# Gate and up products of the last feed-forward: full fp32 products, or three products of split parts

## The chip, the cores and the metric

The kernel runs as one program on one core of a Trainium2 chip. The metric is the device time of one execution in microseconds (us), lower being better. The engines are TensorE (PE: matmuls and transposes through the array, with its weight loads listed apart as PEld), VectorE (DVE), ScalarE (ACT), GpSimd (POOL) and SyncE (SP, which here issues the DMAs).

## What is computed

Four layers, each a cross attention and a feed-forward with a residual and a layer norm, over x of 4 x 256 tokens with 256 features. The change is in the last feed-forward, which multiplies operands that were rounded to 8-bit floats in blocks of 32, each with a scale of its own:

```python
def _mx_dequant(t):            # blocks of 32 along the last dimension
    max_abs = jnp.max(jnp.abs(blocks), axis=-1)
    scales = jnp.maximum(max_abs / 448.0, 1e-30)
    q = (blocks / scales[..., None]).astype(jnp.float8_e4m3fn).astype(jnp.float32)
    return (q * scales[..., None]).reshape(rows, feat)

def _mx_linear(x2d, w):
    return _mx_dequant(x2d) @ _mx_dequant(w).T

gate = _mx_linear(x2d, gate_w)          # 1024 tokens x 256 -> 1024
up = _mx_linear(x2d, up_w)              # 1024 tokens x 256 -> 1024
h = jax.nn.silu(gate) * up
out = _mx_linear(h, down_w)             # 1024 -> 256
```

Before it stands the last cross attention, a linear attention with a sigmoid gate and an output projection; its tokens are worked on in four batches of 256.

## The kernel before

Each engine has one program, written out by hand, and runs it in its written order; semaphores join them. What matters here is the end of each program.

**The last attention** is a loop over four batches b = 0 to 3. In one pass PE makes the denominators and the attention of b, projects query and gate of b + 1 (`query_and_gate`), spreads the inverse denominators over the heads (`spread`, line 1486), transposes a third of the last feed-forward's weights (`pe_turn(pe, "l3", ...)`, b = 1 gate, b = 2 up, b = 3 down; line 475), and projects the output. ACT makes the exponential and the sigmoid of b (lines 1956 and 1963) and then copies the transposed weights out of PSUM (`copy_out`, line 489); PE may run two groups of transposes ahead of these copies. DVE makes the inverse denominators (lines 2718 to 2720), the shares and the product (2729, 2733), the next query's features (2708) and adds the projected output into `x_t` (2742). GpSimd has rounded the weights earlier.

**Before the feed-forward** PE transposes the first 512 tokens back to token rows (line 1537), ACT copies them (1977), DVE rounds them (`tokens_quantised(0)`, through `mx_quant`, lines 2199 to 2216, with `ln_xc_of` 2059 between its steps), PE transposes them again (`quantised_turned`, line 1544) and ACT copies them into `xq_t` (`quantised_copied`, line 1983).

**The feed-forward** goes over eight tiles t of 128 tokens. `gate_up(t)` makes gate into PSUM banks 0 and 1 and up into banks 2 and 3: four outputs of 512 columns, each a sum over KC = 2 products of a 128 x 128 token tile and 128 x 512 weights, thus 8 products a tile. There is one set of these four banks, so `gate_up(t)` waits for the product of tile t - 1 (`m_mul`). ACT applies silu to the gate (`gate_act`, line 1998), DVE multiplies (`product`, line 2766) and rounds the hidden tile (`mx_quant`), GpSimd puts the scale back on (line 933), PE transposes it (`hidden_turned`, line 1573), ACT copies it (line 2005), PE makes `down(t)` of 8 products with 256 columns each, and DVE adds the residual (`result`, line 2790). PE's order in pass t is hidden_turned(t), down(t - 1), gate_up(t + 2); DVE's is product(t + 2) with its rounding, then result(t). The last tile is handled in two halves (lines 2780, 1596, 2017). The tokens of the second half are rounded on DVE after product(1) (`tokens_quantised(1)`) with their last steps on GpSimd (937, 938, 933), and are transposed in PE's pass t = 2, in two pieces around hidden_turned(2) and down(1). All matmuls pass through the helper `mm`, line 959.

Of the kernel before, what the change touches and what calls it, by code (L numbers as in the profile page):

```python
# [13 lines left out]
ALU = mybir.AluOpType  # L14
# [10 lines left out]
P = 128  # L25
D = 256
# [37 lines left out]
def build(nc, a, out, stop=None):  # L64
# [5 lines left out]
    with ExitStack() as ctx:  # L70
# [3 lines left out]
        def sem(name):  # L74
            return ctx.enter_context(nc.semaphore(name))
# [134 lines left out]
        def part_weights(b):  # L210
# [81 lines left out]
        lx_share = c([KC, SEQ])  # L292
        lx_o = c([2, KC, SEQ])
        c = Cut(c3.at / 256)
        wt_l3 = [c([KC, H3]), c([KC, H3]), c([8, D])]
        assert c.at / 256 <= late_at
        c = Cut(0)
        mxq = c([8 * D])
        mx_s = c([2, 96])
        xn_tok = c([TT, D])  # L300
        xq_t = c([KC, TOK])
        h_tok = c([2, H3])
        h_act = c([H3])
        hq_t = c([2, 8, P])
        x_tok = c([TT, D])
        res = c([2, D])


        dve_step, act_step, pool_step = sem("dve_step"), sem("act_step"), sem("pool_step")
# [39 lines left out]
            "lx_made", "lx_copied", "lx_min_r", "lx_exp_r", "lx_keys", "lx_sum", "lx_bd"))  # L349
        lx_qg, lx_qmin_r, lx_act, lx_qf, lx_dens, lx_inverse, lx_att, lx_or, lx_x = (sem(n) for n in (  # L350
            "lx_qg", "lx_qmin_r", "lx_act", "lx_qf", "lx_dens", "lx_inverse", "lx_att", "lx_or", "lx_x"))
        xt_turned, xt_copied, xq_ready, xq_turned, xq_copied = (sem(n) for n in (
            "xt_turned", "xt_copied", "xq_ready", "xq_turned", "xq_copied"))
        res_copied = sem("res_copied")
        m_gu, m_act, m_mul, m_ht, m_htc, m_o, m_res = (sem(n) for n in (
            "m_gu", "m_act", "m_mul", "m_ht", "m_htc", "m_o", "m_res"))
        stored = [sem("stored_even"), sem("stored_odd")]
# [40 lines left out]
        def mark(name, f):  # L398
            first = len(groups)
            f()  # L400
            marks[name] = (first, len(groups))
# [22 lines left out]
        def three(ws, wts, h, wait, fixed):  # L424
            turn_in(h, ws[0], wts[0], wait, fixed)
            turn_in(h, ws[1], wts[1], wait, fixed)
            turn_out(h, ws[2], wts[2], wait, fixed)
# [12 lines left out]
            turn_in(D, lx_nat[1], lx_t[1], (load["l3x"], 16 * 5), 0)  # L440
            turn_in(D, lx_nat[2], lx_t[2], (load["l3x"], 16 * 5), 0)
        mark("lx", lx)
        mark("l3", lambda: three(w_l3, wt_l3, H3, (mx_fixed, 12), 0))

        by_dve = [g % 2 == 1 and not marks["l1"][0] <= g < marks["small"][1] and g < marks["l3"][0] for g in range(len(groups))]

# [510 lines left out]
        def _(pe):  # L957
# [590 lines left out]
            def gate_up(t):  # L1548


                if t:
                    pe.wait_ge(m_mul, t)
                else:
                    pe.wait_ge(xt_copied, 2)
                    pe.wait_ge(res_copied, 2)
                pe.wait_ge(xq_copied, 2 * (t // 4) + 2)
                for n in range(4):

                    j, c2_ = divmod(n, 2) if t < TT - 1 else (n % 2, n // 2)
                    for k in range(KC):  # L1560
                        last = mm(ps[:, 2 * j + c2_, :], xq_t[:, k, t * P:(t + 1) * P],
                                  wt_l3[j][:, k, c2_ * 512:(c2_ + 1) * 512], k == 0, k == KC - 1)
                    if n % 2 or t == TT - 1:
                        last.then_inc(m_gu, 1)

            def hidden_turned(t):

# [9 lines left out]
            def down(t):  # L1577
                pe.wait_ge(m_htc, t + 1)

                if t == 0:  # L1580
                    pe.wait_ge(res_copied, 4)
                elif t < TT - 2:
                    pe.wait_ge(m_res, t)
                for k in range(8):
                    last = mm(ps[:, down_bank(t), 0:D], hq_t[:, t % 2, k, :], wt_l3[2][:, k, :], k == 0, k == 7)
                last.then_inc(m_o, 1)
# [37 lines left out]
            gate_up(1)  # L1624
            for t in range(TT - 1):
                if t == 2:
                    pe.wait_ge(res_copied, 4)
                    quantised_turned(1, 0, 7)
                hidden_turned(t)

                if t:
                    down(t - 1)
                else:
                    pe.wait_ge(xt_copied, 4)
                    tokens_turned_back(x_t, 1, (6, 7))
                if t == 2:
                    pe.wait_ge(xq_copied, 3)
                    quantised_turned(1, 1, 7)
                if t + 2 < TT:
                    gate_up(t + 2)  # L1640
# [8 lines left out]
        def _(act):  # L1649
# [300 lines left out]

            copy_out(act, "lx", False)
            ln_sq_of("l3x", 1)
            act.wait_ge(load["l3x"], 16 * 5)
            for b in range(BATCH):
                act.wait_ge(lx_qmin_r, b + 1)
                act.activation(lx_qmin[:, b % 2], lx_qmin[:, b % 2], ACT.Exp).then_inc(lx_act, 1)
                if b == 0:
                    ln_sd_of("l3x", 1)
                act.wait_ge(lx_qg, 2 * b + 2)
                if b >= 2:  # L1960
                    act.wait_ge(lx_or, b - 1)
                for o in range(KC):
                    last = act.activation(lx_gate[:, b % 2, o, :], ps[:, 1, o * SEQ:(o + 1) * SEQ], ACT.Sigmoid,
                                          bias=bg[:, o:o + 1])
                last.then_inc(lx_act, 1)
                if b == 3:
                    ln_sd_of("l3", 0)
                if b:
                    copy_out(act, "l3", False, (b - 1, BATCH - 1))
                if b == 2:  # L1970
                    ln_sq_of("l3", 0)
# [8 lines left out]
            def quantised_copied(n, bank):  # L1980
                h, k = divmod(n, 2)
                act.wait_ge(xq_turned, n + 1)
                act.activation(xq_t[:, k, tok(h)], ps[:, bank, :], ACT.Copy).then_inc(xq_copied, 1)

            for k in range(KC):
                tokens_copied(k, xn_tok, k, xt_copied)
            for k in range(KC):
                tokens_copied(2 + k, x_tok, 2 + k, res_copied)
            ln_sq_of("l3", 1)
            ln_sd_of("l3", 1)  # L1990
            for k in range(KC):
# [27 lines left out]

            gate_act(0)  # L2020
            for k in range(KC):
                tokens_copied(4 + k, xn_tok, 6 + k, xt_copied)
            for t in range(1, TT - 1):
                gate_act(t)
                if t == 3:
                    quantised_copied(2, 7)
                hidden_copied(t - 1)
                if t == 1:
                    for k in range(KC):
                        tokens_copied(6 + k, x_tok, 6 + k, res_copied)  # L2030
                if t == 3:
                    quantised_copied(3, 7)
            last_gate(0)
# [7 lines left out]
        def _(dve):  # L2041
# [661 lines left out]
            def query_features(b):  # L2703
                dve.wait_ge(lx_act, 2 * b + 1)
                if b >= 2:
# [2 lines left out]
                STT(lx_q[:, b % 2], ps[:, 0, :].rearrange("p (k t) -> p k t", k=KC), 0.0, lx_qmin[:, b % 2], ALU.max,  # L2708
                    ALU.add).then_inc(lx_qf, 1)

            query_negative(0)
            query_features(0)
            ln_diag_of("l3x", 1)
            for b in range(BATCH):
# [28 lines left out]
                if b % 2:  # L2743
                    dve.wait_ge(lx_x, b + 1)
                    dve.sem_inc(x_ready, 1)


            def tokens_quantised(h, **parts):
# [2 lines left out]
                return mx_quant(v, mxq[:, 4 * D * h:4 * D * h + 4 * D], mx_s[:, 0, 64:96], mx_s[:, 1, 64:96], 32, step,  # L2751
                                **parts)

            dve.wait_ge(xt_copied, 2)
            tokens_quantised(0, between=lambda: ln_xc_of("l3", 1)).then_inc(xq_ready, 1)
            ln_diag_of("l3", 1)
            ln_xn_of("l3", 1)

            def product(t):
# [31 lines left out]

            product(0)
            product(1)
            dve.wait_ge(xt_copied, 4)
            dve.wait_ge(xq_ready, 1)
            tokens_quantised(1, rounded=False).then_inc(xq_ready, 1)
            for t in range(TT - 2):
                if t < TT - 3:
                    product(t + 2)
                else:  # L2800
                    last_product(0)
                    last_product(1)
                result(t)
            result(TT - 2)
            result(TT - 1)

# [27 lines left out]
```

## Time and profile before

| | us |
|---|---|
| median of 3 runs | 1015.25 (1014.58 to 1015.99) |
| the profiled execution, whole | 1018.44 |
| its span in the trace | 1016.7 |
| PE busy, share of the span | 864.5 (85%) |
| DVE busy | 716.9 (71%) |
| ACT busy | 453.4 (45%) |
| GpSimd busy | 164.7 (16%) |

All times of single instructions are from this one profiled execution, in microseconds from the start of its span. A busy share is a mean over stages with different limits; the stage of the change is the last 130 us, and is read there by itself. PE's clock is granted at one of two levels, 2.4 GHz (shown as 1.00) and 1.2 GHz (0.50); its mean over this execution is 0.837.

### The profile page before, as it was taken

The page shows a single profiled execution, that of the slowest core. Times are in us where ns is not written, and L with a number is a line of the kernel's source. Part 1 is how long each engine was busy: PE and PEld are TensorE (multiplying, and loading weights), DVE is VectorE, ACT ScalarE, POOL GpSimd, SP SyncE. Part 2 cuts the span into 40 slices and gives each one's busy share as a digit, 9 for nine tenths or more (in the row PEclk, how much of TensorE's full clock was granted, in tenths as well). Part 3 has the DMA queues.
Part 4 walks back from the last instruction along what each step waited for, and adds up shares of the span by engine and source line. Part 5 has one row for each costly group of instructions (what it writes and reads, how often), then busy time and mean ns, then how long its engine had stood idle before and what let it go on. Part 6 is the DMA issues. An engine that isn't in the chain of part 4 may idle for free.

```text
span 1016.7 us, 11697 instructions
## 1 busy us (share of the span) xinstructions
PE 864.5 (85%) x4246; PEld 515.2 (51%) x4246; DVE 716.9 (71%) x962; ACT 453.4 (45%) x695; POOL 164.7 (16%) x251
## 2 busy tenths in 40 slices
PE   5989894489889999999899777777778989889898
PEld 3434662244645555554455434444445657754566
DVE  1776558964457887777668898889985545358777
ACT  2214446642324332222123499888995434532111
POOL 1000000000005424333400062111110000001412
PEclk9899885579979999999899955555558999979999
DMA  8602002100132222141021899987771100000000
GB/s 264 201 2 46 1 0 46 24 2 7 15 50 38 34 33 36 43 65 16 0 47 20 168 170 162 167 154 128 141 140 32 32 0 1 1 1 1 10 11 21
DMA packets 211612, 59.14 MB, mean 58 GB/s; under 512 B 192398, under 2 KB 209892, under 8 KB 211556
## 3 DMA queue, kind: packets, MB, share of 16 engines
q1 hardware_dynamic: 211444, 58.23, 29.8%
q8 instruction: 34, 0.56, 0.2%
q10 hardware_dynamic: 112, 0.17, 0.1%
q14 instruction: 22, 0.18, 0.1%
HBM read 20.62 MB, written 1.05 MB: 21 GB/s over the span
## 4 chain that ended last, share of the span: by engine, by line
PE 55%; DVE 25%; ACT 9%; issue 8%; DMA 1%; POOL 1%; ACTq 1%; DVEq 0%; POOLq 0%
PE ps L959 50%; DVE arena L2640 2%; ACT xc L1924 2%; PE ps L1402 2%; DVE arena L2274 1%; PE ps L475 1%; ACT sq L1924 1%; DVE arena L2204 1%; PE ps L1090 1%; DVE xc L2446 1%; ACT arena_split L1839 1%; DVE sq L2553 1%; DVE sq L2550 1%; DVE xn_t L2075 1%; DVE arena L2188 1%
## 5 line engine op out<-in xcount | busy, mean ns | idle before, releaser
L959 PE MATMUL ps<-arena 128*128 128x16 f16 (+8 forms) x1776 | 265.5, 320 | 50.6 <-ACT xc L1924 22.1
L959 PE MATMUL ps<-arena_split 128*128 128x512 f32 (+6 forms) x736 | 200.4, 436 | 18.6 <-DVE arena_split L2452 5.7
L959 PEld LDWEIGHTS ps<-arena 128*128 128x128 f16 (+4 forms) x1776 | 131.9, 129 | 157.7 <-issue 101.8
L959 PEld LDWEIGHTS ps<-arena_split 128*128 128x128 f32 (+6 forms) x736 | 134.8, 196 | 91.0 <-issue 40.8
L2640 DVE TENSOR_REDUCE arena<-ps 128x1 f32<-128x1024 f32 x128 | 152.3, 1220 | 18.6 <-PE ps L959 17.5
L1924 ACT ACTIVATE xc<-ps,arena 128x1024 int16<-128x1024 f32 x86 | 103.2, 1207 | 13.0 <-POOL arena L916 12.5
L959 PE MATMUL ps<-sq,arena 128*64 128x256 f32 (+3 forms) x256 | 80.9, 515 | 8.0 <-DVE sq L2553 8.0
L865 POOL TENSOR_SCALAR arena<-arena 128x512 f32<-128x512 f32 x12 | 23.1, 1922 | 249.5 <-DVE arena L2468 249.5
L916 POOL TENSOR_SCALAR arena<-arena 128x1 f32<-128x1 f32 x128 | 33.9, 264 | 182.1 <-DVE arena L2640 181.8
L1691 ACT ACTIVATE act_buf<-ps 128x512 f32<-128x512 f32 (+2 forms) x34 | 20.3, 597 | 90.9 <-PE ps L959 90.8
L959 PE MATMUL ps<-mean_w,sq 128*128 128x1 f32 x240 | 35.2, 277 | 21.3 <-ACT sq L1656 21.3
L1924 ACT ACTIVATE sq<-ps,arena 128x1024 int16<-128x1024 f32 x42 | 50.5, 1207 | 5.7 <-POOL arena L916 5.5
L959 PEld LDWEIGHTS ps<-sq,arena 128*64 128x64 f32 (+3 forms) x256 | 30.1, 166 | 43.2 <-issue 31.2
L959 PEld LDWEIGHTS ps<-mean_w,sq 128*128 128x128 f32 x240 | 35.0, 229 | 29.5 <-ACT sq L1656 27.6
L933 POOL TENSOR_TENSOR arena<-arena 128x1024 f32<-128x1024 f32 (+1 forms) x9 | 17.5, 1949 | 186.3 <-DVE arena L2212 186.1
L959 PE MATMUL ps<-x_t,mean_w 128*128 128x512 f32 x64 | 37.9, 723 | 7.8 <-DVE x_t L2296 4.3
L959 PE MATMUL ps<-xn_t,arena 128*128 128x256 f32 (+2 forms) x112 | 39.9, 505 | 0.0
L2384 DVE TENSOR_TENSOR hid_buf<-ps,act_buf 128x512 f32<-128x512 f32 (+2 forms) x18 | 12.4, 690 | 33.8 <-ACT act_buf L1691 33.5
L1830 ACT ACTIVATE act_buf<-ps 128x512 f32<-128x512 f32 x16 | 9.6, 599 | 56.4 <-PE ps L959 56.4
L1839 ACT ACTIVATE arena_split<-xc 128x1024 fp32r<-128x1024 f32 x16 | 16.9, 1059 | 39.3 <-DVE xc L2446 39.3
L475 PE MATMUL ps<-ident,arena 128*128 128x128 f32 (+4 forms) x122 | 22.8, 344 | 13.6 <-DMA arena<-in_x 6.5
L2452 DVE TENSOR_TENSOR arena_split<-xc,arena_split 128x1024 fp32r<-128x1024 f32 x16 | 21.1, 1317 | 18.7 <-ACT arena_split L1839 18.7
(298 smaller groups left out, 1344.5 us busy)
## 6 DMA issues: line engine op xcount, KB each, us to landing
arena<-in_L_ffn_w SPq DMA_DIRECT2D x4, 640.0 KB, 6.0
arena_split<-arena_split SPq DMA_DIRECT2D x59, 32.0 KB
arena<-in_x SPq DMA_DIRECT2D x1, 1024.0 KB, 5.6
arena<-in_ctx SPq DMA_DIRECT2D x1, 1024.0 KB, 8.0
arena<-in_L_xattn_Wkv SPq DMA_DIRECT2D x2, 512.0 KB, 4.0
arena<-in_L_ffn_gate_w SPq DMA_DIRECT2D x1, 1024.0 KB, 10.3
arena<-in_L_ffn_up_w SPq DMA_DIRECT2D x1, 1024.0 KB, 12.8
arena<-in_L_ffn_down_w SPq DMA_DIRECT2D x1, 1024.0 KB, 12.5
```

The source lines that it names most:

```text
L475: last = pe.transpose(ps[0:m, 6 + g % 2, col:col + w], src, ident[0:src.shape[0], 0:src.shape[0]])
L865: step(pool.tensor_scalar(qf, qf, 2.0 ** -6, 1.5 * 2.0 ** 20, ALU.max, ALU.mult))
L916: pool.tensor_scalar(A["bias"][:, b:b + 1], A["nm"][:, b:b + 1], A["sq"][:, t, i:i + 1], math.log(255.0), ALU.mult, ALU.add).then_inc(att_ ...
L933: return pool.tensor_tensor(v, v, scale.unsqueeze(2).to_broadcast([P, n, MX_BLOCK]), ALU.mult)
L959: return pe.matmul(o, l, r, start=start, stop=stop)
L1402: last = pe.transpose(ps[:, 7, :].bitcast(BF16)[:, k * P:(k + 1) * P], y[:, k * P:(k + 1) * P], ident_b[:, :])
L1691: act.activation(act_buf[0:r, u % 2, :], ps[0:r, 2 * (u % 2), :], func, scale=1.0 if scale is None else scale[0:r, :]).then_inc(act_ready, 1)
L1839: act.activation(moe["xe_parts"][:, n % 2, 0], moe["xe"], ACT.Copy).then_inc(moe_xh, 1)
L1924: act.activation(probs(u).rearrange("p (a b) -> p a b", a=2), ps[:, score_banks(u), :], ACT.Exp, bias=att_small["bias"][:, u % 3:u % 3 + 1 ...
L2384: return TTN(hid, up, s, ALU.mult)
L2452: TTN(parts[:, n % 2, 1], moe["xe"], parts[:, n % 2, 0], ALU.subtract).then_inc(moe_xl, 1)
L2640: dve.tensor_reduce(A["nm"][:, b:b + 1], ps[:, score_banks(u), :], AX.XY, ALU.max, negate=True).then_inc(att_max, 1)
```

## The change

Gate and up become three products of parts. Each weight matrix and the rounded tokens are split into a high part, which is the value as ScalarE writes it into the type float32r (`fp32r` in the trace), and a low part, which is the value less the high part, by VectorE, again in float32r. Then x w is made as x_high w_high + x_high w_low + x_low w_high, 24 products a tile in place of 8. The products of `down` stay as they were.

The transposed gate and up weights are first copied to `w3_turned`. In the attention's loop `weight_high(b - 2)` (two ScalarE instructions of 128 x 1024) and `weight_low(b - 2)` (two VectorE instructions of 128 x 1024) stand in passes b = 2 (gate) and b = 3 (up). The tokens' low parts are four VectorE instructions of 128 x 512, `quantised_low`, of which two stand ahead of the first tile, one after result(0), and one after product(3), ahead of result(1). The copies `quantised_copied` write the high parts in place of the plain values. In the first tile of each half (t = 0 and 4) the products with the low part of the tokens come last of all, so that tile's first `m_gu` comes after 20 of its 24 products.

```diff
-        wt_l3 = [c([KC, H3]), c([KC, H3]), c([8, D])]
+        wt_l3 = [c([KC, H3], F32R), c([KC, H3], F32R), c([8, D])]
...
-        xq_t = c([KC, TOK])
+        xq_high = c([KC, TOK], F32R)
...
+        xq_rest = c([KC, TOK], F32R)
+        assert c.at <= c3.at
+        w3_turned = Cut(late_at)([2, KC, H3])
+        w3_rest = Cut(late_at)([2, KC, H3], F32R)
...
@@ gate_up(t), tensor @@
-                    pe.wait_ge(xt_copied, 2)
-                    pe.wait_ge(res_copied, 2)
-                pe.wait_ge(xq_copied, 2 * (t // 4) + 2)
-                for n in range(4):
-
+                    pe.wait_ge(tok_copied, 4)
+                pe.wait_ge(l3_high, WEIGHTS3 + 2 * (t // 4) + 2)
+                pe.wait_ge(l3_low, WEIGHTS3)
+                late = t % 4 == 0
+                if not late:
+                    pe.wait_ge(l3_low, WEIGHTS3 + 2 * (t // 4) + 2)
+                x, y = xq_high[:, :, t * P:(t + 1) * P], xq_rest[:, :, t * P:(t + 1) * P]
+
+                def columns(n):
                     j, c2_ = divmod(n, 2) if t < TT - 1 else (n % 2, n // 2)
+                    return ps[:, 2 * j + c2_, :], j, slice(c2_ * 512, (c2_ + 1) * 512)
+
+                def leading(n):
+                    o, j, at = columns(n)
                     for k in range(KC):
-                        last = mm(ps[:, 2 * j + c2_, :], xq_t[:, k, t * P:(t + 1) * P],
-                                  wt_l3[j][:, k, c2_ * 512:(c2_ + 1) * 512], k == 0, k == KC - 1)
+                        mm(o, x[:, k, :], wt_l3[j][:, k, at], k == 0, False)
+                        mm(o, x[:, k, :], w3_rest[:, j, k, at], False, False)
+
+                def remaining(n):
+                    o, j, at = columns(n)
+                    for k in range(KC):
+                        last = mm(o, y[:, k, :], wt_l3[j][:, k, at], False, k == KC - 1)
                     if n % 2 or t == TT - 1:
                         last.then_inc(m_gu, 1)
+
+                for n in range(4):
+                    leading(n)
+                    if not late:
+                        remaining(n)
+                if late:
+                    pe.wait_ge(l3_low, WEIGHTS3 + 2 * (t // 4) + 2)
+                    for n in range(4):
+                        remaining(n)
...
@@ the attention's loop, scalar @@
+            def weight_high(j):
+
+                act.wait_ge(*copied(marks["l3"][0] + 4 * j + 3))
+                for k in range(KC):
+                    act.activation(wt_l3[j][:, k, :], w3_turned[:, j, k, :], ACT.Copy).then_inc(l3_high, 1)
+
...
                 if b == 3:
                     ln_sd_of("l3", 0)
+                if b >= 2:
+                    weight_high(b - 2)
                 if b:
                     copy_out(act, "l3", False, (b - 1, BATCH - 1))
...
@@ the attention's loop, vector @@
+            def weight_low(j):
+
+                for k in range(KC):
+                    dve.wait_ge(l3_high, KC * j + k + 1)
+                    TTN(w3_rest[:, j, k, :], w3_turned[:, j, k, :], wt_l3[j][:, k, :], ALU.subtract).then_inc(l3_low, 1)
+
...
                 if b % 2:
                     dve.wait_ge(lx_x, b + 1)
                     dve.sem_inc(x_ready, 1)
+                if b >= 2:
+                    weight_low(b - 2)
...
+            def quantised_low(n, bank):
+                h, k = divmod(n, 2)
+                dve.wait_ge(l3_high, WEIGHTS3 + n + 1)
+                TTN(xq_rest[:, k, tok(h)], ps[:, bank, :], xq_high[:, k, tok(h)], ALU.subtract).then_inc(l3_low, 1)
+
...
             ln_diag_of("l3", 1)
+            for k in range(KC):
+                quantised_low(k, 4 + k)
             ln_xn_of("l3", 1)
...
+                if t == 1:
+                    quantised_low(3, 7)
                 result(t)
+                if t == 0:
+                    quantised_low(2, 7)
```

The rest of the diff renames semaphores (`xt_copied` and `res_copied` become one counter, `tok_copied`; `xq_copied` becomes `l3_high`) with the counts that belong to them, and lets PE's second piece of `quantised_turned` in pass t = 2 wait for quantised_low(2), which reads the same PSUM bank.

## Rows read from the trace of the kernel before

**Rows 1.** The page: 40 slices of the span, and the chain that ended last.

```profile
PE   5989894489889999999899777777778989889898
...
PEclk9899885579979999999899955555558999979999
...
PE 55%; DVE 25%; ACT 9%; issue 8%; DMA 1%; POOL 1%; ACTq 1%; DVEq 0%; POOLq 0%
```

**Rows 2.** The chain of waits, 885 to 907 us (start, length, what).

```profile
887.08 0.20 DVE arena L2718
...
888.17 1.11 PE ps L1486 x4
```

**Rows 3.** DVE in order of time: start, length, instruction, [idle before it <- who ended that].

```profile
885.84 0.68 DVE L2742 TENSOR_TENSOR x_t<-ps,x_t 128x512 f32<-128x512 f32 x1
...
894.97 0.69 DVE L2742 TENSOR_TENSOR x_t<-ps,x_t 128x512 f32<-128x512 f32 x1 [0.51 <-PE ps L959]
...
896.52 1.22 DVE L2199 TENSOR_REDUCE arena<-arena 128x32 f32<-128x1024 f32 x1 [0.86 <-ACT arena L1977]
...
917.96 1.22 DVE L2766 TENSOR_TENSOR arena<-ps,arena 128x1024 f32<-128x1024 f32 x1 [6.82 <-PE ps L959]
...
926.51 1.22 DVE L2766 TENSOR_TENSOR arena<-ps,arena 128x1024 f32<-128x1024 f32 x1 [0.23 <-PE ps L959]
...
951.52 0.42 DVE L2790 TENSOR_TENSOR arena<-ps,arena 128x256 f32<-128x256 f32 x1
...
967.86 1.23 DVE L2766 TENSOR_TENSOR arena<-ps,arena 128x1024 f32<-128x1024 f32 x1 [7.24 <-PE ps L959]
...
990.28 1.23 DVE L2766 TENSOR_TENSOR arena<-ps,arena 128x1024 f32<-128x1024 f32 x1 [2.43 <-PE ps L959]
```

**Rows 4.** ACT in order of time, at the places of the new copies, and a silu.

```profile
879.88 1.08 ACT L489 ACTIVATE arena<-ps 128x512 f32<-128x512 f32 x2 [8.42 <-PE ps L475]
...
888.66 0.26 ACT L1661 ACTIVATE sd<-ps,eps_col 128x4 f32<-128x4 f32 x1
890.17 0.60 ACT L489 ACTIVATE arena<-ps 128x512 f32<-128x512 f32 x1 [1.25 <-PE ps L475]
...
964.37 1.02 ACT L1998 ACTIVATE arena<-ps 128x1024 f32<-128x1024 f32 x1 [3.85 <-PE ps L959]
```

**Rows 5.** PE in order of time: split products, full products, first and fifth tile.

```profile
809.79 3.59 PE L959 MATMUL ps<-arena_split 128*128 128x512 f32 x15
...
909.68 8.18 PE L959 MATMUL ps<-arena 128*128 128x512 f32 x16
...
919.24 7.14 PE L959 MATMUL ps<-arena 128*128 128x512 f32 x16 [0.51 <-DVE arena L2766]
...
953.53 1.97 PE L1573 MATMUL ps<-ident,arena 128*128 128x128 f32 x8 [3.04 <-POOL arena L933]
...
960.66 7.11 PE L959 MATMUL ps<-arena 128*128 128x512 f32 x16 [0.78 <-ACT arena L1983]
```

**Rows 6.** Split operands in the other stages: count, duration ns min/median/max, first and last start.

```profile
L1839 ACT ACTIVATE arena_split<-xc x16: 1047/1059/1063, 282.4 to 528.1; 128x1024 fp32r<-128x1024 f32 x16
L2452 DVE TENSOR_TENSOR arena_split<-xc,arena_split x16: 1224/1226/1984, 283.5 to 529.2; 128x1024 fp32r<-128x1024 f32 x16
...
L2341 DVE TENSOR_TENSOR arena_split<-ps,arena_split x8: 691/691/693, 265.9 to 496.4; 128x512 fp32r<-128x512 f32 x8
```

**Rows 7.** Stretches: us, PE busy, PEld, DVE, ACT, POOL, granted clock, DMA share, GB/s.

```profile
888.00:891.50 3.50, 3.33 (x16) 3.10 (x16) 2.28 (x5) 1.98 (x4) 0.00 (x0) 0.51 0.00 0
...
909.60:912.00 2.40, 2.40 (x4) 1.01 (x3) 1.22 (x1) 0.51 (x1) 0.00 (x0) 0.51 0.00 0
...
953.00:956.40 3.40, 2.87 (x11) 2.69 (x12) 3.23 (x6) 0.86 (x1) 0.47 (x1) 0.51 0.07 25
...
968.00:1001.00 33.00, 33.00 (x118) 20.21 (x117) 27.07 (x35) 6.31 (x7) 5.74 (x3) 1.00 0.04 12
```

**Rows 8.** GpSimd in order of time: the scale put back on a hidden tile.

```profile
998.68 1.91 POOL L933 TENSOR_TENSOR arena<-arena 128x1024 f32<-128x1024 f32 x1 [9.30 <-DVE arena L2212]
```

More of the change, by code:

```diff
@@ L351, in build @@
             "lx_qg", "lx_qmin_r", "lx_act", "lx_qf", "lx_dens", "lx_inverse", "lx_att", "lx_or", "lx_x"))
-        xt_turned, xt_copied, xq_ready, xq_turned, xq_copied = (sem(n) for n in (
-            "xt_turned", "xt_copied", "xq_ready", "xq_turned", "xq_copied"))
-        res_copied = sem("res_copied")
+        xt_turned, tok_copied, xq_ready, xq_turned, l3_high, l3_low = (sem(n) for n in (
+            "xt_turned", "tok_copied", "xq_ready", "xq_turned", "l3_high", "l3_low"))
+        WEIGHTS3 = 2 * KC
         m_gu, m_act, m_mul, m_ht, m_htc, m_o, m_res = (sem(n) for n in (
@@ L442, in build @@
         mark("lx", lx)
-        mark("l3", lambda: three(w_l3, wt_l3, H3, (mx_fixed, 12), 0))
+        mark("l3", lambda: three(w_l3, [w3_turned[:, 0], w3_turned[:, 1], wt_l3[2]], H3, (mx_fixed, 12), 0))
         by_dve = [g % 2 == 1 and not marks["l1"][0] <= g < marks["small"][1] and g < marks["l3"][0] for g in range(len(groups))]
@@ L1580, in down @@
                 if t == 0:
-                    pe.wait_ge(res_copied, 4)
+                    pe.wait_ge(tok_copied, 8)
                 elif t < TT - 2:
@@ L1626, in _ @@
                 if t == 2:
-                    pe.wait_ge(res_copied, 4)
+                    pe.wait_ge(tok_copied, 8)
                     quantised_turned(1, 0, 7)
@@ L1633, in _ @@
                 else:
-                    pe.wait_ge(xt_copied, 4)
+                    pe.wait_ge(tok_copied, 6)
                     tokens_turned_back(x_t, 1, (6, 7))
                 if t == 2:
-                    pe.wait_ge(xq_copied, 3)
+                    pe.wait_ge(l3_low, WEIGHTS3 + 3)
                     quantised_turned(1, 1, 7)
@@ L1982, in quantised_copied @@
                 act.wait_ge(xq_turned, n + 1)
-                act.activation(xq_t[:, k, tok(h)], ps[:, bank, :], ACT.Copy).then_inc(xq_copied, 1)
+                act.activation(xq_high[:, k, tok(h)], ps[:, bank, :], ACT.Copy).then_inc(l3_high, 1)
             for k in range(KC):
-                tokens_copied(k, xn_tok, k, xt_copied)
+                tokens_copied(k, xn_tok, k, tok_copied)
             for k in range(KC):
-                tokens_copied(2 + k, x_tok, 2 + k, res_copied)
+                tokens_copied(2 + k, x_tok, 2 + k, tok_copied)
             ln_sq_of("l3", 1)
@@ L2021, in _ @@
             for k in range(KC):
-                tokens_copied(4 + k, xn_tok, 6 + k, xt_copied)
+                tokens_copied(4 + k, xn_tok, 6 + k, tok_copied)
             for t in range(1, TT - 1):
@@ L2029, in _ @@
                     for k in range(KC):
-                        tokens_copied(6 + k, x_tok, 6 + k, res_copied)
+                        tokens_copied(6 + k, x_tok, 6 + k, tok_copied)
                 if t == 3:
@@ L2752, in tokens_quantised @@
                                 **parts)
[L2754 removed]
+            def quantised_low(n, bank):
+                h, k = divmod(n, 2)
+                dve.wait_ge(l3_high, WEIGHTS3 + n + 1)
+                TTN(xq_rest[:, k, tok(h)], ps[:, bank, :], xq_high[:, k, tok(h)], ALU.subtract).then_inc(l3_low, 1)
+            dve.wait_ge(tok_copied, 2)
             tokens_quantised(0, between=lambda: ln_xc_of("l3", 1)).then_inc(xq_ready, 1)
             ln_diag_of("l3", 1)
+            for k in range(KC):
+                quantised_low(k, 4 + k)
             ln_xn_of("l3", 1)
@@ L2793, in _ @@
             product(1)
-            dve.wait_ge(xt_copied, 4)
+            dve.wait_ge(tok_copied, 6)
             dve.wait_ge(xq_ready, 1)
```

## The prediction

> **What bounds the kernel now.** I read the page first. PE is busy nearly all the time and holds 55% of the chain that ended last, but the last fifth of the span has busy tenths of 8 and 9 with dips, and the clock line falls to 7 in one slice there [rows 1]. So the share over the whole span says little, and I went through the last 130 us by the chain of waits and by each engine's order in time. Four parts with different limits come out.
>
> (A) 885 to 896: in the attention's last pass a short DVE step (887.08) releases PE's `spread` at 888.17 [rows 2]; in PE's program 16 weight transposes and the output projection follow. DVE adds that projection at 894.97 and starts rounding the tokens at 896.52, having waited 0.86 for ACT's copies [rows 3].
> (B) 896.5 to 918: rounding on DVE, then PE: gate_up(0) from 909.68, and product(0) at 917.96 after 6.82 us of idle DVE [rows 3, 5]. Here PE is the bound.
> (C) 917.96 to 951.52: DVE is never idle by more than the 0.23 us ahead of product(1) [rows 3]. DVE is the bound for three hidden tiles and the second half's tokens.
> (D) 951.52 to the end: PE waits for GpSimd's scale of tile 2 until 953.53, then for ACT's copy before gate_up(4) at 960.66 [rows 5]. Product(4) comes at 967.86 after 7.24 us of idle DVE [rows 3]. From 968 to 1001 PE is busy 33.00 of 33.00 us at full clock [rows 7]; the two tiles from product(4) to product(6) at 990.28 take 22.42, or 11.21 each. After product(6) its rounding, the two halves of the last tile and their rounding follow on DVE, so the rest hangs on product(6).
>
> Only in B and D can faster products shorten anything; what is added on DVE in A is paid in full.
>
> **The price of a product.** Each full product is two records. Sixteen of them, gate_up(1), take 7.14 us, 0.59 of it the last one's own length, so 0.43 a record and 0.86 a product [rows 5]. The second feed-forward already runs products of split parts of the same size: 15 records start within 3.59 - 0.39 = 3.20 us, 0.228 each [rows 5]. A tile's 8 x 0.86 = 6.9 becomes 24 x 0.228 = 5.5 us: 1.4 us less at full clock, 11 us over eight tiles if PE were the bound everywhere.
>
> **Part A, the weights' parts.** On ACT each of four copies costs 1.06, on DVE each of four subtractions 1.23 [rows 6]. The gate's copies (2.1 us) fall into ACT's 8.42 us of idleness before 879.88: nothing. The up weights' copies start after the root at 888.66 to 888.92 and end at 891.05, where ACT's first weight copy stands at 890.17 [rows 4]: 0.9 us, if DVE had not moved that copy further, which it does. The subtractions of the gate weights start behind the addition at 885.84, at about 886.45, and end 2.4 us later (two of 1.23, overlapping by 0.08) at 888.85. The step of 887.08 waits behind them: +1.8 us on PE's path. The weight copy then comes at about 892, so ACT's own 0.9 is covered.
>
> The clock: from 888.0 to 891.5 PE runs at 0.51, after a time in which it stood still several times, and rises after this busy stretch [rows 7]. With `spread` at 890 in place of 888.2 the stretch holds half as much work, and I expect the low level to last into the transposes and the projection. That costs 0 to 0.9 us; I take 0.4, between the two. The projection is then 2.2 us later. The up weights' subtractions follow the addition of 894.97, whose semaphore passes at 895.7: 895.7 + 2.2 + 2.4 = 900.3, against a start of the rounding at 896.52. That is +3.8, less 0.1 of a wait before `ln_xc_of` that goes: **+3.7 us** (3.2 to 4.2).
>
> **Part B, the first tile.** The low parts of the tokens, 0.69 each [rows 6], run on DVE beside PE's norm rows and end before the norm product needs its operand; nothing. gate_up(0) thus starts at 913.4. Before, it took 8.28 us to product(0), of which 2.3 were at 0.51 of the clock (909.6 to 912.0) [rows 5, 7]. Now ACT's silu needs the 20th product, not the 24th: 20 x 0.228 = 4.6, its drain, silu of 1.02 [rows 4] and two hand-overs come to 5.9, and about 2 us at the low level add 1.0: 6.9. **-1.4 us** (-2.4 with no low clock; +1.5 if one more stretch like that of 888 to 891.5 lies over it). Product(0) is 2.3 us later than before.
>
> **Part C.** DVE-bound, with the same instructions; GpSimd stands in the same place relative to them. gate_up(1) now ends well inside DVE's rounding, so only the wait goes: **-0.2 us**. The 1.4 us that each of gate_up(1) to (3) loses become idle time of PE. quantised_low(2) sits after result(0) at 951.52: 0.69 on DVE, covered by the time to product(4), where DVE was idle 7.24 us [rows 3]; quantised_low(3) likewise. Were that cover gone they would cost 1.4.
>
> **Part D.** From 951.52 GpSimd, the transposes of tile 2, down(1), the second token piece and ACT's copy stay. gate_up(4) to product(4) was 7.2 us (960.66 to 967.86) and becomes 5.9: **-1.3**. But 953.0 to 956.4 ran at 0.51 after PE had stood for 3.04 us [rows 5, 7]. Now gate_up(3) ends earlier against DVE and that gap is about 4.7 us, so I expect more of the transposes and of down(1) at the low level: **+0.7** (0 to +2).
>
> In the steady tiles PE's own work falls from 11.2 to 9.8, but another loop comes up: product(t), its rounding (8.4 from 990.28 to GpSimd's start at 998.68), GpSimd 1.91 [rows 8], a hand-over (10.37 in all), then transposes and down (11.21 - 6.9 = 4.3), gate_up 5.5, drain and hand-over 0.2: 20.4 us for product(t) to product(t + 2). Before, the same loop came to 10.4 + 4.3 + 6.9 + 0.2 = 21.8, hidden under PE's 22.42. So two tiles gain **-2.0 us**, not 2.8. DVE itself (8.4 and a result of 0.42, 8.8 a tile [rows 3]) stays under it. After product(6) DVE sets the pace: unchanged.
>
> Sum: +3.7 - 1.4 - 0.2 - 1.3 + 0.7 - 2.0 = **-0.5 us**. The profiled execution took 1018.44, 3.2 above the median; the sum is a difference within its 1016.7 us of span, and I put it on the median: 1015.25 - 0.5 = 1014.7.
>
> The clock is where a rule speaks against the change. The rows show it low after each pause of PE. The Trainium skill (TensorE: Matmul & The Clock Gate, "Why this matters for your kernels") says to avoid pauses between bursts of matmuls, since the throughput then drops. This change makes PE's bursts shorter between the same waits. By that rule the sum would lean to the rival below; the trace agrees as far as low stretches go, and shows that a pause of 0.8 us before gate_up(4) cost no clock.
>
> **Rivals.** Slower: the clock. Each us of PE work on the path that falls to the low level costs 0.5 us. If one more stretch of 3.4 us lies over gate_up(0) (+1.7) and the one before gate_up(4) is also 3.4 us longer (+1.7 in place of +0.7), and the transposes of A stay low (+0.5), the sum is -0.5 + 3.2 = +2.7: 1018.0. For it: the low stretches stand exactly at these three places already. Against: split products keep PE as busy as full ones, and after the longest pause the clock was back at 912.0, within 5.8 us of PE's first work (906.2), a first tile or less. It decides once more than about 5 us of further PE work on the path is at the low level.
>
> Faster: the clock does not get worse (-0.4 in A, -0.7 in D) and gate_up(0) meets the full level early (-1.0): -2.6, giving 1012.6. For it: part B starts 3.7 us later against the clock's changes, which could as well help.
>
> Not as said: float32r products with stationary tokens could run at the full products' 0.43 each. Then 24 cost 10.3 against 6.9, some +20 us. The split products of rows 5 exclude this nearly.
>
> **How the numbers follow.** Forecast (1013.3 to 1017.1 by its own bounds) 0.56; slower 0.20 at 1018.0; faster 0.22 at 1012.6; not as said 0.02. A measurement of this kernel tells about 0.2% (2.0 us) from no change, so faster means below 1013.2 and slower above 1017.3. The range reaches both rivals' times, 1012.2 to 1018.1, and leaves out what goes beyond them.
>
> **What would show it.** In the new trace: split products 0.228 apart; `spread`(3) about 1.8 us later; token rounding at about 900.3; product(0) near 920.3; DVE without a gap from there to result(0), about 33.3 us; product(4) to product(6) 20.4 us with PE waiting 0.7 for GpSimd in every other tile; 24 us from product(6) to the last addition. The prediction fails first where the clock does something else in A, B or at the start of D, or if DVE or GpSimd slow each other in C at other places than before.

## The result: 1011.8 us, and where the difference lies

The changed kernel takes 1011.79 us in the median of 22 runs (1008.99 to 1019.8), against 1016.56 for the kernel before in the 22 runs beside them. The ratio is 0.9956, with a 95% interval of 0.9942 to 0.9971: 4.5 us faster (2.9 to 5.9; the plain medians lie 4.8 apart), where the forecast said 0.5 us and the range began at 1012.2. The kernel before was itself 1.3 us slower here than the 1015.25 from which the forecast started. A second set of runs gave the ratio 0.9962 (0.9945 to 0.9979). So the kernel became faster by more than 0.2%, which had a chance of 0.22.

The page of the changed kernel, busy time and clock, and the chain that ended last; they answer [rows 1]:

```profile
span 1008.9 us, 11843 instructions
...
PE 846.8 (84%) x4310; PEld 521.8 (52%) x4310; DVE 723.8 (72%) x970; ACT 457.0 (45%) x699; POOL 164.8 (16%) x251
...
PEclk9899995589979999999899955555558999979899
...
PE 52%; DVE 27%; ACT 10%; issue 8%; DMA 1%; POOL 1%; ACTq 1%; DVEq 0%; POOLq 0%
```

The span is 7.8 us shorter than the 1016.7 of before. DVE in time order says where: the query features of the last batch start at 877.92, against 885.23 before. Up to there the changed kernel differs only in where the transposed weights are stored and in the two ScalarE copies of the gate weights, and these cost nothing: from the third batch's query features to the last batch's it takes 14.20 us in all four profiles of the changed kernel below, and in three of the four of the kernel before. In the first profile of before it took 15.88, with the granted clock at 0.50 from 871.0 to 874.4. So 7.3 of the 7.8 us lie ahead of every instruction that can matter. The rows from there on answer [rows 3], with the new instructions L2750 and L2800 among them:

```profile
877.92 0.69 DVE L2743 SCALAR_TENSOR_TENSOR arena<-ps,arena 128x512 f32<-128x512 f32 x1 [4.57 <-ACT arena L1989]
878.53 0.68 DVE L2783 TENSOR_TENSOR x_t<-ps,x_t 128x512 f32<-128x512 f32 x1
879.13 2.35 DVE L2750 TENSOR_TENSOR arena_split<-arena,arena_split 128x1024 fp32r<-128x1024 f32 x2
...
893.18 1.21 DVE L2234 TENSOR_REDUCE arena<-arena 128x32 f32<-128x1024 f32 x1
...
913.02 1.22 DVE L2816 TENSOR_TENSOR arena<-ps,arena 128x1024 f32<-128x1024 f32 x1 [5.35 <-ACT arena L2033]
...
946.44 0.43 DVE L2840 TENSOR_TENSOR arena<-ps,arena 128x256 f32<-128x256 f32 x1
946.78 0.68 DVE L2800 TENSOR_TENSOR arena_split<-ps,arena_split 128x512 fp32r<-128x512 f32 x1
...
962.17 1.23 DVE L2816 TENSOR_TENSOR arena<-ps,arena 128x1024 f32<-128x1024 f32 x1 [5.00 <-ACT arena L2033]
...
982.76 1.22 DVE L2816 TENSOR_TENSOR arena<-ps,arena 128x1024 f32<-128x1024 f32 x1 [1.96 <-PE ps L963]
```

And PE, for [rows 5]:

```profile
905.44 7.42 PE L963 MATMUL ps<-arena_split 128*128 128x512 f32 x24
...
914.30 5.85 PE L963 MATMUL ps<-arena_split 128*128 128x512 f32 x24 [0.57 <-DVE arena L2816]
...
948.45 1.97 PE L1599 MATMUL ps<-ident,arena 128*128 128x128 f32 x8 [5.07 <-POOL arena L937]
...
972.53 1.09 PE L1599 MATMUL ps<-ident,arena 128*128 128x128 f32 x8 [0.60 <-POOL arena L937]
```

From the query features to the end the two profiles read 131.5 and 131.0 us: -0.5, to the tenth what the sum gave. Its larger terms hold too. Query features to first rounding +4.0 (forecast +3.8), rounding to product(0) -1.6 (-1.5), product(0) to result(0) -0.1 (-0.2), product(3) to product(4) -1.2 (-1.3, with its later start), product(4) to product(6) -1.8 (-2.0). Yet the ratio of the runs says 4.5 us. That contradiction is what the experiments are for.

### The profile page after: what moved, and what is told of

It reads as the page before. It is cut to its first block, busy times and chain, and to the rows that moved or that the text cites. A ratio compares the mean times of both kernels' runs of the same rounds, so it can differ in the third digit from the quotient of the medians.

```text
span 1008.9 us, 11843 instructions
## 1 busy us (share of the span) xinstructions
PE 846.8 (84%) x4310; PEld 521.8 (52%) x4310; DVE 723.8 (72%) x970; ACT 457.0 (45%) x699; POOL 164.8 (16%) x251
## 4 chain that ended last, share of the span: by engine, by line
PE 52%; DVE 27%; ACT 10%; issue 8%; DMA 1%; POOL 1%; ACTq 1%; DVEq 0%; POOLq 0%
PE ps L963 47%; DVE arena L2675 2%; ACT xc L1950 2%; PE ps L1406 2%; DVE arena L2239 1%; ACT sq L1950 1%; DVE arena L2309 1%; PE ps L479 1%; DVE arena L2234 1%; PE ps L1094 1%; DVE xc L2481 1%; ACT arena_split L1865 1%; DVE arena L2241 1%; DVE arena L2246 1%; DVE arena L2247 1%
## 5 line engine op out<-in xcount | busy, mean ns | idle before, releaser
L963 PE MATMUL ps<-arena_split 128*128 128x512 f32 (+6 forms) x928 | 247.0, 428 | 19.6 <-DVE arena_split L2487 5.8
L963 PE MATMUL ps<-arena 128*128 128x16 f16 (+8 forms) x1648 | 207.3, 298 | 49.4 <-ACT xc L1950 22.1
L963 PEld LDWEIGHTS ps<-arena_split 128*128 128x128 f32 (+6 forms) x928 | 170.0, 194 | 101.4 <-issue 42.5
L963 PEld LDWEIGHTS ps<-arena 128*128 128x128 f16 (+5 forms) x1648 | 107.1, 124 | 126.6 <-issue 71.9
L2487 DVE TENSOR_TENSOR arena_split<-xc,arena_split 128x1024 fp32r<-128x1024 f32 x16 | 21.0, 1315 | 18.7 <-ACT arena_split L1865 18.7
```

The lines of the kernel that those rows point to most:

```text
L963: return pe.matmul(o, l, r, start=start, stop=stop)
L2487: TTN(parts[:, n % 2, 1], moe["xe"], parts[:, n % 2, 0], ALU.subtract).then_inc(moe_xl, 1)
```

## The experiments

Theory 1: TensorE's clock falls and rises at other places in each execution. I call one such sequence of low stretches a clock order. Each profile is one draw of it, the draw of before was a good one for this part, and in typical executions the changed kernel gains more there. Theory 2: the sum is right in general and the runs differ by chance. Theory 3: one of the sum's bare terms, those without the clock, is mis-sized.

I read each profile in the same stages, all between starts of VectorE instructions: Q, the last batch's query features; R, the first rounding of the tokens; p0, p3, p4, p6, product(0) to product(6); end.

**The changed kernel again,** with no edit.

> The changed kernel again. Two executions were profiled so far: from the last batch's query features (VectorE, 885.23 us before, 877.92 us after) to the end of the span they show 131.5 us before and 131.0 us after, while the medians of 22 executions lie 4.5 us apart. Theory 1 (the clock): this last part is some 4 us shorter in a typical execution and the one profile fell on an unlucky order of low-clock stretches (23.8 us of them in this part, against 20.4 us before); expected here 125 to 129 us for this part, and a ratio of 0.994 to 0.997. Theory 2 (my sum was right and the rest is chance of the runs): again 130 to 132 us, and a ratio of 0.997 to 1.001.

Ratio 0.9962 (0.9945 to 0.9979). Q to end is 129.1 us, just above theory 1's 125 to 129 and below theory 2's 130 to 132.

**The kernel before again,** as the control.

> The kernel before against itself, as the control: ratio 0.999 to 1.001. Its last part from the last batch's query features to the end was 131.5 us in the one profile; theory 1 lets it vary by 1 to 3 us with the order of the low-clock stretches and expects 130 to 134; theory 2 expects 131 to 132 each time.

Ratio 0.9995 (0.9978 to 1.0012), and Q to end is 134.3 us, just above even theory 1's range, where the first profile had 131.5. The same instructions differ by 2.8 us in this part alone.

**Two more profiles of each.**

> A third profile of the kernel before, to see how far its last part moves with the order of the low-clock stretches. It was 131.5 us with 20.5 us of low clock in it and 134.3 us with 27.3. If my one profile was the good end of the draw, this one is above 131.5 (132 to 135); if it was typical, near 131.5.

> A third profile of the changed kernel. Its last part was 131.0 us and 129.1 us, both with 23.9 us of low clock. The two executions with one clock order in both kernels (low from 880.0 and 880.5 on) lie 5.2 us apart, the two others 0.5. Expected 128.5 to 131.5; product(4) to product(6) again 20.6, product(3) to product(4) 14.3 to 14.9.

> A fourth profile of the kernel before: as the third, above 131.5 us in its last part if the first was a lucky one. From the query features to the first rounding of the tokens: 11.3 us with the clock full at the start, 12.6 with it low.

> A fourth profile of the changed kernel, last part 128.5 to 131.5 us. From the query features to the first rounding: 14.5 us with the clock low from the start on, 15.3 with it full at the start. The mean of four against four should lie 3 to 5 us below the kernel before if the difference of the medians comes from this part.

The expectation that the first profile of before was the lucky end was only half right: the third one is lower still, 130.9. All eight, in us, with the low clock between Q and the end in brackets:

| profile | Q to R | R to p0 | p0 to p3 | p3 to p4 | p4 to p6 | Q to end |
|---|---|---|---|---|---|---|
| before, first | 11.29 | 21.45 | 33.90 | 16.00 | 22.42 | 131.5 (20.5) |
| before, again | 12.61 | 21.30 | 33.88 | 17.62 | 22.42 | 134.3 (27.3) |
| before, third | 11.24 | 19.96 | 33.89 | 16.95 | 22.42 | 130.9 (17.1) |
| before, fourth | 12.62 | 21.30 | 33.89 | 17.62 | 22.42 | 134.3 (27.3) |
| changed, first | 15.26 | 19.84 | 34.36 | 14.79 | 20.59 | 131.0 (23.9) |
| changed, again | 14.47 | 19.11 | 34.36 | 14.33 | 20.61 | 129.1 (23.9) |
| changed, third | 14.47 | 19.12 | 34.37 | 14.35 | 20.59 | 129.1 (23.9) |
| changed, fourth | 14.47 | 19.08 | 34.37 | 14.34 | 20.59 | 129.0 (23.9) |

The means are 132.75 and 129.55: -3.2 us in this part. The columns where PE's clock stays full (p4 to p6) or DVE alone sets the pace (p0 to p3) repeat to 0.02; the others move by 0.5 to 1.6 us. Two of four profiles of before and three of four of the changed kernel have one and the same order, low from just after Q; between these the difference is 134.3 - 129.0 = 5.3 us. The first two profiles (I predicted from the first, and compared the two first) are the pair with the smallest gain but one. This speaks for theory 1, though four profiles each don't tell how often each order comes. Below, "the common order" is this one.

**What that common order does to the weights' parts.** PE in the fourth profile of before, then DVE there, then the same of the changed kernel's fourth:

```profile
880.75 3.79 PE L959 MATMUL ps<-arena 128*128 128x8 f32 x12 [0.72 <-DVE arena L2708]
884.33 1.06 PE L1486 MATMUL ps<-ident,arena 128*128 128x128 f32 x4
...
949.48 1.97 PE L1573 MATMUL ps<-ident,arena 128*128 128x128 f32 x8 [3.04 <-POOL arena L933]
951.25 5.77 PE L959 MATMUL ps<-arena 128*128 128x256 f32 x16
```

```profile
880.01 0.69 DVE L2708 SCALAR_TENSOR_TENSOR arena<-ps,arena 128x512 f32<-128x512 f32 x1 [4.57 <-ACT arena L1956]
...
882.67 0.19 DVE L2718 TENSOR_SCALAR arena<-ps 128x32 f32<-128x32 f32 x1 [1.37 <-PE ps L959]
```

```profile
878.56 3.78 PE L963 MATMUL ps<-arena 128*128 128x8 f32 x12 [0.72 <-DVE arena L2743]
882.37 1.12 PE L1490 MATMUL ps<-ident,arena 128*128 128x128 f32 x4
...
946.80 1.97 PE L1599 MATMUL ps<-ident,arena 128*128 128x128 f32 x8 [5.07 <-POOL arena L937]
948.56 4.32 PE L963 MATMUL ps<-arena 128*128 128x256 f32 x16
```

```profile
877.81 0.69 DVE L2743 SCALAR_TENSOR_TENSOR arena<-ps,arena 128x512 f32<-128x512 f32 x1 [4.57 <-ACT arena L1989]
...
881.28 0.18 DVE L2759 TENSOR_SCALAR arena<-ps 128x32 f32<-128x32 f32 x1
```

At the low level PE needs 3.8 us for denominators and attention, against 2.0 at full clock in the first profile (885.98 to 888.0). `spread` then stands 4.32 us after Q in before anyway, because PE itself is late. In the changed kernel it stands 4.56 us after Q: the 2.35 us of the gate weights' subtractions cost 0.2, where the sum charged 1.8. DVE had 1.37 us of waiting there. The up weights' subtractions cost the rest, 1.6; Q to R grows by 1.85, not 3.8.

At tile 2's transposes (949.48 and 946.80) PE's pause grew from 3.04 to 5.07 us, as predicted, but the low stretch behind it did not. Stretches from there to gate_up(4), fourth profiles of before and changed (us, busy times, granted clock):

```profile
949.40:958.20 8.80, 7.97 (x28) 6.63 (x28) 6.90 (x9) 1.62 (x2) 1.94 (x2) 0.65 0.00 0
```

```profile
946.80:954.00 7.20, 6.51 (x28) 5.62 (x28) 6.93 (x9) 1.62 (x2) 0.00 (x0) 0.78 0.00 0
```

The same work takes 1.6 us less in the changed kernel, down(1) alone 4.32 against 5.77. The low stretch itself was shorter: the granted clock is 0.51 from 946.6 to 950.0 and 1.00 from there to 954.0, while in before it is 0.50 from 948.8 to 955.6. The pauses hid little of either, 0.2 and 0.7 us. What made the stretch shorter is not shown, and in the first pair it was the other way round (3.4 us in before, 6.8 in the changed kernel). The length of a pause alone does not settle it: the changed kernel's pause of 3.23 us before tile 0's transposes is in its first and its fourth profile alike, and the clock behind it stays 1.00 in the first (923.38 to 930.0) and is 0.50 in the fourth (922.7 to 926.1).

**The split alone.** The products become 8 full ones of the high parts; the low parts are left out of the computation.

```diff
-                        mm(o, x[:, k, :], wt_l3[j][:, k, at], k == 0, False)
-                        mm(o, x[:, k, :], w3_rest[:, j, k, at], False, False)
+                        last = mm(o, x[:, k, :].bitcast(F32), wt_l3[j][:, k, at].bitcast(F32), k == 0, k == KC - 1)
...
-                for k in range(KC):
-                        last = mm(o, y[:, k, :], wt_l3[j][:, k, at], False, k == KC - 1)
```

> All the split work stays (copies, subtractions, their places), but gate and up are 8 full fp32 products of the high parts instead of 24 split products; the low parts are left out of the computation. It gives the price of the split alone. My sum puts it at +3.7 us before the first tile and nothing after: 3 to 5 us above the kernel before, ratio 1.003 to 1.005. If the price of the split is smaller than thought (1 to 2 us, ratio 1.001 to 1.002), then part A of the sum is what failed; if it is 3.7, the gain from faster products is larger than thought.

Ratio 1.0023 (1.0006 to 1.0041): +2.3 us (0.6 to 4.2); the middle lies below the 3 to 5 expected, though the interval reaches into them. Q to R is 14.44, the same as in the changed kernel. So by the ratios the split costs about 2 us, and the split products bring about 6, from 1.0023 to 0.996. The one profile has Q to end at 134.5, hardly above the 134.3 of before in the common order: R to p0 (20.27) and p3 to p4 (16.54) are about 1 us shorter each, though the products are the old ones. Its low clock in this part is 23.9 us against 27.3, so in this profile the clock gives back what the split costs.

**The weights' low parts on GpSimd.**

```diff
+            for j in range(2):
+                for k in range(KC):
+                    pool.wait_ge(l3_high, KC * j + k + 1)
+                    pool.tensor_tensor(w3_rest[:, j, k, :], w3_turned[:, j, k, :], wt_l3[j][:, k, :],
+                                       ALU.subtract).then_inc(lx_bd, 1)
...
-                if b >= 2:
-                    weight_low(b - 2)
```

> The four subtractions of the weights (2 x 2.35 us on VectorE in the trace of after) are moved to GpSimd, which is idle until 921 us. By my sum they cost 3.8 us of path on VectorE: expected 3 to 4 us below the changed kernel, about 1008 us, ratio to before 0.991 to 0.993. If they cost only their bare effect on the clock or are hidden, 0 to 1 us below the changed kernel.

Ratio 0.9953 (0.9933 to 0.9972), not to be told from the changed kernel's: the 0.991 to 0.993 expected did not come. Q to R alone did what the edit was for: it is 12.60, as in before with the clock low from just after Q (12.61). GpSimd needs 4.66 us for each pair, and nobody waits for it:

```profile
869.75 4.66 POOL L939 TENSOR_TENSOR arena_split<-arena,arena_split 128x1024 fp32r<-128x1024 f32 x2 [82.47 <-ACT arena_split L1990]
888.88 4.68 POOL L939 TENSOR_TENSOR arena_split<-arena,arena_split 128x1024 fp32r<-128x1024 f32 x2 [14.47 <-ACT arena_split L1990]
```

So the whole price of part A in that order is 1.9 us, and it was the subtractions' place that made it. Most of it was lost again behind R: R to p0 is 20.14 against 19.1, with 3.2 us of the first tile at the low level where it was 1.1 in the changed kernel's fourth profile, p3 to p4 is 14.91 against 14.34, and Q to end 128.8 against 129.0. This profile also lost 3.4 us ahead of Q, where the last pass took 17.55 in place of 14.20 with 6.8 us of low clock in it; the variant below with both edits also has some there (15.88). Whether the edit has a part in that is open.

**TensorE kept busy in its pauses,** in both kernels: three full products before the last norm's variance, three behind it, four before tile 2's transposes, into a PSUM bank that is free there.

```diff
+            def kept_busy(bank, n):
+                for _ in range(n):
+                    mm(ps[:, bank, :], mean_w[:, :], ctx_t[:, 0, 0:HALF], True, True)
+
             ln_mean_of("l3", 1)
+            pe.wait_ge(tok_copied, 1)
+            kept_busy(0, 3)
             ln_var_of("l3", 1)
+            kept_busy(0, 3)
...
+                if t == 2:
+                    pe.wait_ge(m_htc, t)
+                    kept_busy(4, 4)
                 hidden_turned(t)
```

> The changed kernel with ten extra full products on TensorE, whose results nobody reads, in three of its pauses: three before the last norm's variance, three after it, four before the transposes of tile 2. It leaves the result as it is. By the traces the pause before gate_up(0) is followed by 10.2 us at the low level, of which about 5 us are TensorE work on the path, and the one before tile 2's transposes by 3.4 us. If the clock is what these waits cost: first rounding to product(0) falls from 19.1-19.8 to about 17.2 us, product(3) to product(4) from 14.3-14.8 to about 13 us, and the kernel is 3 to 4 us below the changed one (ratio to before 0.992 to 0.994). If the clock is no matter there, no change or the extra products' own delay (0 to +2 us).

> The kernel before with the same ten extra products in the same places. With the low level out of both, the difference to the changed kernel with them is the bare one of the sum: +3.2 (weights' parts) - 1.4 (first tile) - 0.2 - 1.3 (fifth tile) - 1.8 (steady tiles), about -1.5 us. Theory 1 (the clock makes the rest, the kernel before loses more to it than its one profile showed): about -1.5 us between these two. Theory 3 (a bare term is mis-sized): the -4 us of the plain pair stay.

The changed kernel goes to 0.9938 (0.9916 to 0.9961), the kernel before to 0.996 (0.9943 to 0.9977). The low clock in the kernel before falls from 27.3 to 6.8 us in this part, and the time saved is as much as the whole change brought. For the changed kernel the ratio is in the range expected, but the step below it is about 2 us and not the 3 to 4 expected. Stages:

| profile | Q to R | R to p0 | p3 to p4 | p4 to p6 | Q to end |
|---|---|---|---|---|---|
| before, kept busy | 12.61 | 18.82 | 14.65 | 22.42 | 128.8 (6.8) |
| changed, kept busy | 14.47 | 18.23 | 12.82 | 20.61 | 126.7 (10.2) |

Both have one clock order up to R. R to p0 of the changed kernel missed the 17.2 expected: a stretch of 3.4 us at the low level is left there, and the extra products ran in it and delayed the transposes. The transposes of tile 2 now run at full clock in both, 1.09 us in place of 1.97. Changed kernel, kept busy:

```profile
900.64 4.52 PE L963 MATMUL ps<-ctx_t,mean_w 128*128 128x512 f32 x6
904.99 1.04 PE L1548 MATMUL ps<-ident,arena 128*128 128x128 f32 x8
...
943.06 3.60 PE L963 MATMUL ps<-ctx_t,mean_w 128*128 128x512 f32 x8
948.29 1.09 PE L1599 MATMUL ps<-ident,arena 128*128 128x128 f32 x8 [1.64 <-POOL arena L937]
```

The two now lie 2.1 us apart by the profiles, where the plain pair in its common order lay 5.3 apart. By the ratios it is 2.2, in place of about 4; but the plain medians (1013.40 and 1010.05) say 3.3, and the two intervals overlap, so the runs alone exclude neither 1.5, which theory 1 expected, nor 4, which theory 3 did. The case against theory 3 rests on the stages, where every bare term can be read by itself. By them about half of the difference is the clock. The bare terms p3 to p4 (-1.83, forecast -1.95 from p3) and p4 to p6 (-1.8, forecast -2.0) hold.

**Both edits.**

> Both edits on the changed kernel: weights' low parts on GpSimd and TensorE kept busy. If they add up: 1 to 3 us below the one with TensorE kept busy alone, ratio to before about 0.989 to 0.992.

1008.76 us, ratio 0.9922 (0.9899 to 0.9946), Q to end 123.0, R to p0 17.54 with no low clock in it. The step below the changed kernel kept busy (1010.05) is 1.3 us by the medians, inside the 1 to 3 expected, and by the intervals not to be told from nothing; the ratio is just above the 0.989 to 0.992 expected. The profiles lie 3.7 us apart (126.7 and 123.0), of which about 1 is another clock order at the start: Q to R is 11.46 here, with the clock full until 885.1. The median is the lowest of all these kernels, 0.8% below before and 0.3 to 0.4% below the changed one by the middle values, whose intervals just touch.

**Fewer products.** The third product is left out of the computation, 16 a tile.

```diff
-                        mm(o, x[:, k, :], w3_rest[:, j, k, at], False, False)
+                        last = mm(o, x[:, k, :], w3_rest[:, j, k, at], False, k == KC - 1)
...
-                        last = mm(o, y[:, k, :], wt_l3[j][:, k, at], False, k == KC - 1)
```

> The third product (low part of the tokens with the high part of the weights) is left out of the computation, 16 products a tile instead of 24; all else as in the changed kernel. TensorE's work falls by 8 x 0.228 = 1.8 us a tile. If the loop product, rounding, GpSimd, transposes, down, gate and up, product binds the steady tiles (20.6 us for product(4) to product(6)), these fall once by 1.8 to 18.8 us. If TensorE alone binds, they would fall by 3.6 to 17.0, where VectorE's 2 x 8.8 = 17.6 would stop them.

p4 to p6 took 20.38 us, neither 18.8 nor 17.0, and the ratio is 0.9969 (0.9944 to 0.9994): a third of the work gone and no gain. PE now waits longer for GpSimd, and the clock falls in the steady tiles too, where it was full in every other profile:

```profile
968.39 4.07 PE L963 MATMUL ps<-arena_split 128*128 128x512 f32 x16
974.87 1.97 PE L1597 MATMUL ps<-ident,arena 128*128 128x128 f32 x8 [2.41 <-POOL arena L937]
...
995.25 1.93 PE L1597 MATMUL ps<-ident,arena 128*128 128x128 f32 x8 [2.39 <-POOL arena L937]
```

Between product(4) and product(6) the transposes take 1.97 in place of 1.09 and the products of down behind them 4.43 in place of 3.62: the 3.4 us at the low level cost 1.7. 20.4 - 1.7 = 18.7, the 18.8 of the loop. So the loop through VectorE and GpSimd binds, as the prediction had it, and the clock takes the gain. The Trainium skill's advice (TensorE: Matmul & The Clock Gate, "Why this matters for your kernels") to avoid pauses between bursts is borne out in these tiles, with pauses of 2.4 us; the first tile's pause of 3.23 us above shows that not every pause costs the clock.

## Why the prediction was wrong, by its own steps

- **The price of a product** (0.228 for 0.86): right. 24 products take 5.85 us with their drain, 7.14 for 8 before.
- **Part A, +3.7 us: mis-sized outside the clock order it was read in.** It came to 4.0 in the first pair of profiles and 1.85 in the common order. The 1.8 us for the gate weights' subtractions assumed that VectorE's step released PE; in the first pair `spread` is 1.6 us later, but where PE runs at the low level, PE is late itself, and 0.2 is left. The ACT copies were hidden, as said.
- **Part B, -1.4:** with the clock kept full or nearly, 18.23 against 18.82, -0.6, and -1.3 with the 17.54 of the last variant, which has no low clock in that stage; -1.6 in the first pair, -2.2 in the common order. Right in its bare size, and again more with the clock.
- **Part C:** right. product(0) to result(0) is 33.42 for 33.56; quantised_low costs 0.48 from p0 to p3 and is covered.
- **Part D, fifth tile:** bare term right (1.83 for 1.95). The +0.7 for the clock was +0.6 in the first pair and has the wrong sign in the common order: p3 to p4 fell by 3.28, that is 1.45 more than the bare term, since the kernel before spent 6.8 us of that stage at the low level and the changed one 3.4. The pause grew as expected (5.07, for 4.7 forecast); that a longer pause makes a longer low stretch for the work behind it did not follow.
- **Part D, steady tiles, -2.0:** 1.83, with PE waiting 0.60 and 0.54 for GpSimd in every other tile. Right. A further 0.28 came at the very end, where the transposes of the last tile's first half no longer wait for PE (four records at 1000.96, four at 1002.16, instead of eight after 1009.05). I had called the tail unchanged.
- **The step that failed over all:** I put a difference read within one execution on the median of the runs, and gave the clock's terms the sizes of that execution. I saw that 1018.44 was 3.2 above the median, yet took it for a plain offset. Most of that offset lies ahead of the change; within the changed part this profile was 1.3 us better than the mean of four. The range took the clock mainly as a danger to the changed kernel. Even with each term at the end of its bounds that favours the change (+3.2 in A, -2.4 in B, no +0.7 in D) the sum is -2.7, so the measured -4.5 lay outside what its terms allowed. The bounds 1013.3 to 1017.1 are not worked out from the terms, and one reading for the rival "slower" is wrong: the longest single pause in its rows is the 3.04 us before 953.53, not the 2.56 us before 906.2. The rival "faster" had the right kind of cause, an order of the clock that suits the changed kernel, but was built from a small gain in it alone and left out that the kernel before can lose 3 us more.

What stays open: the last part explains -3.2 us in the means of four profiles and the ratios say -4.5 and -3.9, whose intervals hold 3.2; the share of each clock order isn't known better than that. The time up to Q went from 877.8 to 885.2 us. Its mean is 2.9 us lower in the changed kernel's four profiles than in the four of before, but over all fourteen profiles, those of the variants included, the means are 880.5 (changed, nine) and 881.0 (before, five), so nothing shows that the change acts there. Nor is it shown what sets a clock order.

## What to carry to other kernels

Where a profile shows TensorE's clock falling in the stage of a change, the terms of a sum that have low clock in them are draws: profile the kernel before several times, and price the stage in each order it shows, for both kernels. Work added on one engine costs only what the other engine's lateness leaves of it, and that lateness depends on the clock. Shortening TensorE's bursts between fixed waits can lose in clock what it gains in work; ten useless products in the pauses were worth as much to the kernel before as the change itself. Moving the added work to an idle engine took its whole price out of its own stage, and still no gain could be told in the total, since the clock behind it moved too: read such an edit to the end of the kernel, not in its stage alone.

## What I had not expected of the hardware

- The same instructions took 130.9 to 134.3 us in the last part alone (before, four profiles), and 19.96 to 21.45 us in one stage of it.
- Ten products whose results nobody reads made the kernel before 0.4% faster (0.996).
- GpSimd's subtraction of two 128 x 1024 fp32 tensors took 2.36 us (4.66 from the start of the first to the end of the second), VectorE's 1.23; its product with a broadcast operand takes 1.91 [rows 8].
- Sixteen products a tile were no faster than twenty-four (0.9969 against 0.9956).
